# A two-layer hybrid kernel: 23 added constant products in the opening, and two of its three order tables written anew

## The reference, cut to what matters

```python
x = x + conv(group_norm(x))           # 16 graphs of 256 nodes, 16 features, 16 times
    # E = softmax(V_e @ sigmoid(..)), S = softmax(V_s @ sigmoid(prod2 + b_s), axis=1)
    # out = sum_k (cheb[k] * S).T @ x @ Theta[k]; relu; conv over time; + residual; layer norm
t = x as tokens                        # (16, 256 tokens, 256 channels)
t = t + linear_attention(layer_norm(t))   # 16 heads, causal, phi = elu + 1
t = t + ffn(layer_norm(t))                # shared part and top 4 of 16 experts
```

## Time and profile before

| what | value |
|---|---|
| median of 3 runs | 1003.73 us (1002.51 to 1003.75) |
| the profiled execution | 1005.99 us, its span 1004.2 us |
| granted clock, mean over the span | 0.952 |
| PE busy | 941.5 us, 94% |
| DVE busy | 606.8 us, 60% |
| ACT busy | 426.0 us, 42% |
| POOL busy | 210.2 us, 21% |
| the chain that ended last | PE 86%, DVE 6%, ACT 6% |
| first product of `0:gu0` | 188.43 us into the span |

### The profile page before, as it was taken

How to read it: one execution, slowest core, us unless ns; L and a number is a source line. 1 busy time by engine, 2 the same in 40 slices (tenths; PEclk the granted TensorE clock), 3 DMA queues, 4 the chain that set the end, 5 groups by cost and what they waited for, 6 DMA issues and landing times.

```text
span 1004.2 us, 20050 instructions
## 1 busy us (share of the span) xinstructions
PE 941.5 (94%) x8208; PEld 832.8 (83%) x8208; DVE 606.8 (60%) x1630; ACT 426.0 (42%) x808; POOL 210.2 (21%) x184
## 2 busy tenths in 40 slices
PE   4797779999999999999999999999999999999997
PEld 2586556998988989889888898889888888988997
DVE  5548854667576366853777447853768447854532
ACT  3533413452365325741265424752256513632442
POOL 2003200022312023111331123121231113212222
PEclk9689757999999999999999999999999999999999
DMA  9100000000000000000000010000100000000000
GB/s 321 45 1 22 1 1 1 2 23 12 1 11 1 1 33 1 12 1 32 2 12 2 1 33 1 12 2 1 33 1 12 2 12 2 11 1 12 12 12 11
DMA packets 14378, 17.78 MB, mean 18 GB/s; under 512 B 1072, under 2 KB 12720, under 8 KB 14288
## 3 DMA queue, kind: packets, MB, share of 16 engines
q1 hardware_dynamic: 14288, 16.51, 4.9%
HBM read 12.31 MB, written 4.19 MB: 16 GB/s over the span
## 4 chain that ended last, share of the span: by engine, by line
PE 86%; DVE 6%; ACT 6%; issue 1%; POOL 0%; DMA 0%; POOLq 0%; SPq 0%; DVEq 0%; ACTq 0%
PE ring L1305 9%; PE g_ps L501 5%; PE d_ps L501 5%; PE d_ps L503 4%; PE d_ps L502 4%; PE g_ps L503 4%; PE g_ps L502 4%; PE u_ps L501 4%; PE u_ps L502 4%; PE u_ps L503 4%; PE ring L1177 4%; PE num L1206 3%; PE ring L1288 3%; PE ring L501 3%; PE ring L503 3%; PE ring L502 3%
## 5 line engine op out<-in xcount | busy, mean ns | idle before, releaser
L647 POOL TENSOR_TENSOR hl<-hb,hh 128x512 fp32r<-128x512 f32 x96 | 127.2, 1325 | 494.4 <-ACT hh L791 494.4
L1145 DVE TENSOR_TENSOR hb<-sl,u_ps 128x512 f32<-128x512 f32 x88 | 60.2, 684 | 99.9 <-PE u_ps L503 48.4
L791 ACT ACTIVATE hh<-hb 128x512 fp32r<-128x512 f32 x96 | 60.8, 633 | 140.1 <-DVE hb L1149 119.7
L501 PE MATMUL d_ps<-hh,down_h 128*128 128x256 f32 x384 | 114.9, 299 | 1.9 <-POOL hl L647 1.9
L501 PE MATMUL g_ps<-normed_h,gate_h 128*128 128x256 f32 x352 | 109.0, 310 | 3.6 <-DVE scb L1061 3.5
L503 PE MATMUL d_ps<-hh,down_l 128*128 128x256 f32 x384 | 107.5, 280 | 0.0
L502 PE MATMUL d_ps<-hl,down_h 128*128 128x256 f32 x384 | 107.4, 280 | 0.0
L503 PE MATMUL g_ps<-normed_h,gate_l 128*128 128x256 f32 x352 | 100.4, 285 | 0.0
L501 PE MATMUL u_ps<-normed_h,up_h 128*128 128x256 f32 x352 | 100.1, 284 | 0.0
L502 PE MATMUL g_ps<-normed_l,gate_h 128*128 128x256 f32 x352 | 100.1, 284 | 0.0
L502 PE MATMUL u_ps<-normed_l,up_h 128*128 128x256 f32 x352 | 100.1, 284 | 0.0
(11 more groups left out here) (338 smaller groups left out, 2176.3 us busy)
## 6 DMA issues: line engine op xcount, KB each, us to landing
out_x<-kept SPq DMA_DIRECT2D x16, 256.0 KB, 2.1
x_s<-in_x SPq DMA_DIRECT2D x14, 256.0 KB, 3.0
raw_weights<-in_gateT SPq DMA_DIRECT2D x4, 384.0 KB, 9.2
raw_weights<-in_upT SPq DMA_DIRECT2D x4, 384.0 KB, 10.1
raw_weights<-in_down SPq DMA_DIRECT2D x4, 384.0 KB, 12.6
cheb_s<-in_cheb SPq DMA_DIRECT2D x3, 256.0 KB, 4.8
raw_weights<-in_wqkvT SPq DMA_DIRECT2D x2, 384.0 KB, 6.9
shared<-in_x SPq DMA_DIRECT2D x2, 256.0 KB, 2.9
```

Source lines behind the costliest of these rows:

```text
L501: eng.matmul(ps, wh, xh, start=start, stop=False, **how)
L647: pool.tensor_tensor(hl[:, j % 2, :], hb, hh[:, j % 2, :].bitcast(F32), ALU.subtract).then_inc(*ffn_pool.mark(p, f"lo{j}"))
L791: act.activation(hh[:, j % 2, :], hb, ACT.Copy).then_inc(*ffn_act.mark(p, f"hi{j}"))
L1145: dve.tensor_tensor(hb, sl, gate_up(p, j)[1][:, :], ALU.mult).then_inc(*ffn_dve.mark(p, f"h{j}"))
```

## The change

A new chain `warm` has 23 steps `hot0` to `hot22`, each one float32 product of the identity with 256 columns of the constants into `g_ps`, which nothing reads; `gu0` overwrites the bank later. A hot step exists on PE alone, waits for nothing of its own and signals nothing. All 23 stand in `OPENING`, before `0:gu0`. `OPENING` and `BODY` are written anew; `CLOSING` and all other work stay as they were.

```diff
+CHAINS["warm"] = [f"hot{i}" for i in range(23)]
 OPENING = """
-    0:gn 0:xg 1:gn 1:xg 0:xT0 0:M 1:xT0 0:xT1 1:M 0:Y0 0:prod 1:xT1 0:xb 0:Epre 1:Y0 0:Eexp 1:prod 0:Erep 0:lr 1:Epre
...
+    0:gn 1:gn 0:xg 0:hot0 0:hot1 0:hot2 1:xg 0:hot3 0:xT0 0:M 0:xT1 0:Y0 0:hot4 0:prod 0:hot5 1:xT0 0:Epre 1:M 0:hot6
+    0:Eexp 1:xT1 1:Y0 0:hot7 1:prod 1:Epre 0:Erep 1:Eexp 0:lr 0:p2 0:sp0 0:rv0 1:Erep 0:sp1 1:lr 0:st0 0:rv1 1:p2 0:Y1
...
 BODY = """
-    tok0 tok1 +1 lg +1 nrm gn xl0 xg +1 xl1 +1 xT0 r1 M xT1 +1 k0 +1 k1 v1 r2 +2 r3 Y0 +1 q0 v0 kt q1 prod silu r4 +2
...
+    +1 tok0 tok1 lg nrm +1 gn +2 xg xl0 +1 xl1 +1 r1 +2 xT0 M k0 k1 v1 xT1 +1 Y0 r2 q0 r3 v0 kt q1 prod silu +1 r4 +1
...
             def front(p, name):
+                if name in CHAINS["warm"]:
+
+                    pe.matmul(g_ps[:, 0:N], ident, cs[:, 0:N], start=True, stop=True)
+                    return
                 g = room(p)
```

More of the change, by code:

```diff
@@ new lines @@
+    0:Eexp 1:xT1 1:Y0 0:hot7 1:prod 1:Epre 0:Erep 1:Eexp 0:lr 0:p2 0:sp0 0:rv0 1:Erep 0:sp1 1:lr 0:st0 0:rv1 1:p2 0:Y1
+    0:hot8 0:st1 1:sp0 0:xb 1:rv0 0:o0 0:o1 1:sp1 0:tc0 1:st0 0:tc1 1:rv1 0:z1 1:xb 0:z2 1:Y1 0:hot9 0:z3 1:st1 1:o0
+    1:o1 1:tc0 0:tok0 1:tc1 1:z1 0:tok1 0:hot10 2:gn 0:nrm 0:hot11 1:z2 0:xl0 0:xl1 0:hot12 0:hot13 2:xg 0:k0 0:k1
+    0:v1 2:xT0 2:M 0:q0 0:v0 0:kt 0:q1 0:hot14 0:hot15 0:hot16 1:z3 2:xT1 0:hot17 0:dent 2:Y0 0:hot18 2:prod 0:kv
+    2:Epre 2:Eexp 0:rd 0:S00 0:hot19 0:hot20 2:Erep 0:V00 0:S01 0:at0 2:lr 0:V01 0:S10 2:p2 0:V10 0:S11 2:sp0 0:V11
@@ L123 @@
+    2:rv0 0:at1 2:sp1 2:st0 0:wo0 0:wo1 2:rv1 2:Y1 0:hot21 0:tk0 0:exp 0:tk1 0:nrm2 2:st1 2:o0 0:xn0 0:hot22 1:tok0
+    0:xn1 1:tok1 2:o1 0:lg 1:nrm 0:r1 +1 0:r2 1:xl0 1:xl1 +1 2:tc0 +1 0:r3 0:silu 1:k0 1:k1 1:v1 1:q0 1:v0 1:kt 1:q1
+    +1 2:tc1 0:r4 1:dent 1:kv +1 0:cb +2 1:rd +4 1:S00 +1 1:V00 +3 1:S01 +1 1:at0 1:V01 +1 2:xb +2 1:S10 +2 1:V10 +2
+    1:S11 +2 1:V11 +3 1:at1 +1 2:z1 +1 1:wo0 +1 2:z2 +2 1:wo1 +3 1:tk0 1:tk1 +3 1:nrm2 +2 2:z3 +1 1:xn0 +2 1:xn1 +2
+    1:exp +1
 """
 BODY = """
-    tok0 tok1 +1 lg +1 nrm gn xl0 xg +1 xl1 +1 xT0 r1 M xT1 +1 k0 +1 k1 v1 r2 +2 r3 Y0 +1 q0 v0 kt q1 prod silu r4 +2
@@ L127 @@
-    Epre dent cb kv +1 rd +2 Eexp S00 +2 Erep +1 lr +3 p2 +2 sp0 rv0 sp1 +1 st0 V00 +2 rv1 Y1 +3 xb S01 +1 st1 +1 at0
-    +1 o0 +1 o1 V01 +1 S10 +1 tc0 +1 tc1 V10 z1 S11 +1 V11 +2 at1 +1 z2 +1 wo0 +1 wo1 +2 tk0 tk1 +5 nrm2 z3 +1 xn0 xn1
+    +1 tok0 tok1 lg nrm +1 gn +2 xg xl0 +1 xl1 +1 r1 +2 xT0 M k0 k1 v1 xT1 +1 Y0 r2 q0 r3 v0 kt q1 prod silu +1 r4 +1
+    Epre dent cb kv +1 rd +2 Eexp S00 +2 Erep +1 lr +3 p2 +2 sp0 rv0 sp1 +1 st0 V00 +2 rv1 Y1 +3 S01 +2 st1 +1 at0 +1
+    xb +1 o0 o1 tc0 V01 S10 +1 tc1 V10 z1 +1 S11 +1 V11 +2 at1 +1 z2 wo0 wo1 +2 tk0 +2 tk1 +2 nrm2 +2 z3 +2 xn0 xn1
@@ L165, in program @@
         put(int(word.split(":")[0]) if ":" in word else None, word.split(":")[-1])
-    names = [n for c in CHAINS for n in CHAINS[c]]
-    assert sorted(out) == sorted((p, n) for p in range(PAIRS) for n in names)
+    once = [(p, n) for p in range(PAIRS) for c in CHAINS if c != "warm" for n in CHAINS[c]]
+    assert sorted(out) == sorted(once + [(0, n) for n in CHAINS["warm"]])
     for c in CHAINS:
+        if c == "warm":
+            continue
         orders = [[n for q, n in out if q == p and n in CHAINS[c]] for p in range(PAIRS)]
@@ L194 @@
 GROUPS = [f"{b}{lc}" for b in range(2) for lc in range(2)]
-NO_TILE = ["xg", "Eexp", "rv0", "rv1", "nrm", "nrm2", "at0", "at1", "exp", "silu"] + ["V" + g for g in GROUPS] + CHAINS["tail"] + CHAINS["ffn"] + "lg r1 r2 r3 r4 cb".split()
+NO_TILE = ["xg", "Eexp", "rv0", "rv1", "nrm", "nrm2", "at0", "at1", "exp", "silu"] + ["V" + g for g in GROUPS] + CHAINS["tail"] + CHAINS["ffn"] + CHAINS["warm"] + "lg r1 r2 r3 r4 cb".split()
 RING = 4
```

## The result

Four runs of the changed kernel took 985.80 to 989.00 us, median 987.22 us; the kernel before had a median of 1003.74 us beside them. The ratio is 0.984 (95% interval 0.9825 to 0.9857). The profiled execution took 988.29 us with a span of 986.5 us, 17.7 us under the profiled execution of before (1005.99 us). The mean granted clock rose from 0.952 to 0.980.

What follows compares the result with a forecast made beforehand. Bound: the start of feed-forward work (188.43 us) plus nearly fixed PE work. Opening -8.7 and middle -5.5 sum to -14.2 us, from 1005.99 to 991.8, against the median 989.5, said as 990; range 979 to 999.

Steps and rivals of the forecast that it cites:

- rival 2: Whole kernel: the clock holds everywhere, in 24.4 to 58.5 us too, 9.5 us more gain, 980 us; chance 0.16.
- the prediction's own signs of being wrong: Clock mostly full between 24 and 58 us (then nearer 980), or score groups still at 2.09 us (then 997 or more).
- Its signs for the scores: From 110 to 165 us: clock over 0.8 instead of 0.6, `S` at 1.15 us in at least three of four groups.
- Up to 68 us: Opening, `conv` of pair 0: 24.4 to 44.9 us stays at half clock, DVE's `1:M` delays `0:Eexp`; +1.0 us.
- 68 to 95 us: Opening: hot9 saves 1.7 us at the fall at 79.0, `0:z3` on DVE gives back most; -0.5 us.
- 95 to 123 us: Norm and projections of pair 0: `0:xl0` about 2.5 us later, projections mostly at full clock; sum -2.0 us.
- The scores: 123 to 161 us, scores and weighing: about 8.5 us gained, two falls of 3.4 us take back 2.5; -6.0 us.
- 161 to 188 us: End of the opening: hot21 and hot22 save 1.7 us, one product of 0.5 stands on the path; -1.2 us.
- The middle: Behind `gu0`: waits of `gu0` -3.5, `M` -1.5, half the clock falls -2.5, new waits 2; -5.5 us.
- PE idle by 4 to 5 us less: Sign for the middle: PE idles 4 to 5 us less, with the wait on L1061 gone.
- Rival 1: Whole kernel: the clock falls where it fell before, terms from 95 us on worth 2, middle 4; 997 us; chance 0.20.
- Rival 3: Opening: late DVE and POOL queues (`1:z1`, `2:gn`; `1:M`) cost 5.0 us, products don't raise the clock; 1012 us; chance 0.06.

Runs made afterwards that it cites:

- e3_gn_later: The changed kernel with `gn` of the middle's table moved behind two more feed-forward steps; 1013.24 us.
- e4_eexp_first: The changed kernel with only `Eexp` of pair 0 put back ahead of the work of `M` of pair 1 on DVE; 987.46 us.
- e1_no_hot: The changed kernel without its 23 hot products, both new tables kept; 1000.83 us.
- e4_more_hot: The changed kernel with more hot products in the waits of the opening, 64 in all; 980.64 us.
- e2_norm_first: The changed kernel with the norm of pair 0 put back ahead of `1:z1` and `2:gn`, and `0:Eexp` ahead of `1:M`; 991.73 us.
- e1_new_opening: The changed kernel with the old table for the middle, its new opening and products kept; 988.41 us.
- e1_new_body: The kernel before with the new table for the middle, old opening, no hot products; 999.70 us.
- e1_hot_only: The kernel before with the 23 hot products between the same neighbours, both old tables otherwise kept; 997.61 us.

## Why the prediction held, point by point

990 us was forecast and 987.22 measured. The way the change was said to work came about, on the side of rival 2. That the number came so near has some luck in it: the opening gave 14.0 us in the profiles where 8.7 were forecast (`gu0` at 174.5 us, not 179.5), the middle 3.8 where 5.5 were, and the two misses partly cancel. And one of the prediction's own signs of being wrong came: between 24 and 58 us the clock is mostly full, 0.80 on the mean where it was 0.60. Its signs for the scores came as well: 0.91 from 110 to 165 us, three groups of four at 1.15 us, and the wait on L1061 gone.

**What bounds it.** That the time is the start of `gu0` plus a nearly fixed remainder held in every kernel but e3_gn_later: behind `gu0` lie 809.9 to 815.8 us, while `gu0` itself moves by 22 us.

**Up to 68 us: this step failed.** "So I leave the stretch 24.4 to 44.9 at half clock" gave +1.0; the trace has -3.6. After, only 29.5 to 39.9 and 50.0 to 53.4 us are at half clock, 14 us in place of 27. `Erep` is 2.2 us later (28.33 against 26.12), but not for the reason given, the work of `M` ahead of `Eexp` on DVE: without it (e4_eexp_first) it starts no sooner, since `1:Epre` now stands ahead of it on PE and waits for ACT. It runs in 1.06 instead of 1.86 us, `p2` starts only 1.4 us later, and the 12.8 us of `o` shrink to 10.5, since the low stretch no longer meets them. `o` starts 0.4 us later than before, with `sp0` of pair 1 (1.9 us at full clock) now ahead of it and no longer behind, which is most of the rest. The clock came back 5 us earlier than in before, at 39.9 instead of 44.9. The reason given, "what holds PE there is not PE", was true of the waits and wrong of the clock. The size is not one number: the four other profiles give -0.5 to -3.2, and e1_no_hot, which had 20 us at half clock there without a single product, -1.8. e4_more_hot shows the rest of it: with every wait filled, `o` starts at 49.8 us.

**68 to 95 us.** -0.5 forecast, -0.4 measured.

**95 to 123 us.** -2.0 forecast, -2.7 up to the scores. The sum came out, its first part did not: `xl0` was to be 2.5 us later and starts at 100.69 us, 2.6 earlier than before (103.28). Two things stand behind that. 4.0 us were in hand from the first two terms, which leaves it 1.4 later in its own stretch. And the late norm was real, `xl0` waits 1.73 us for it, but it was not what the projections waited for: with the old order `xl0` comes 1.1 us sooner in its stretch and the first projection 0.8 later (e2_norm_first). The stretch of low clock is still there, 10.2 us in place of 13.6.

**The scores.** -6.0 forecast, -4.7 measured. Of the two falls of 3.4 us that were counted, one came, of 10.2 us, and three groups of four ran at 1.15 us. In another execution of the same opening none came (e1_new_opening). This term is therefore not one number: the clock's pattern changes from run to run, as the spread of 985.8 to 989.0 us with clocks of 0.984 and 0.980 shows.

**161 to 188 us.** -1.2 forecast, -2.5 measured; about 1.0 of it is work of pair 1 (`xl0`, `xl1`) that now stands behind `gu0`, and so is no gain. With it counted where it stood, this stretch gave 1.5 and the middle 4.8.

**The middle: this step was mis-sized, and its parts wrong.** -5.5 forecast, -3.8 measured. The two waits went (3.5 and 1.8 us), the falls of the clock went wholly (-5.1 where -2.5 was counted), and the new waits, put at 2, are 4.1 and 3.4 us. The forecast "PE idle by 4 to 5 us less" is refuted: it idles 1.5 us more. That the falls went because of `w11` and `M` was argued from their place behind those waits; every profile with the new body as it is has none, e1_new_body with the old opening too. But in e1_new_opening, with all five waits for `scb` there, one fall is left of three, so the wait alone does not make them; which move removes them was not tried.

**The rivals.** Rival 1 (997, the clock falls where it fell) is what e1_hot_only measured, 997.6, but for the old order, not the new; its sum leaves out the +1.0 of the first term and would be 998 with it. Rival 2 (980, the clock holds everywhere) was reached by e4_more_hot at 980.64 us: the ceiling was about right, and 23 products are too few for it. Rival 3 fell: the products do raise the clock, and undoing its two late queues gains nothing (e2_norm_first, e4_eexp_first).

**The page's rule.** The Trainium skill (TensorE: Matmul & The Clock Gate, Part 1) puts the cost of the ramp below 1% of a typical span. Here the clock falls again and again while PE waits in the opening, and the kernel in which it no longer falls there is 22.4 us faster, 2.1 to 2.5% by its interval (e4_more_hot), of which the new body had given 4.1 by itself (e1_new_body). For one ramp the rule may hold; for falls that repeat in the waits the measurement decides.

## What to carry to other kernels

Where a profile shows half clock, sum it by stretch and ask what PE waits for there: filling those waits with wide products of constants that nothing reads costs about 0.5 us each at full clock, mostly hides in the wait, and makes all real products in the stretch faster. Fill every wait before the bulk of the work starts, instead of choosing places by where the clock fell in one trace, since the pattern changes between executions; the fill is enough when no stretch is left. Here 23 products were worth 6.2 us in an order that was not made for them and 13.6 in one that was.

On one shared order a removed wait tends to come back at the next consumer (`q0`, then `Y0`), and a step moved later on PE is moved on the engine that feeds it too (`gn`).

## What the runs showed of the hardware

- A product of 16 columns does not hold the clock up and one of 256 does, at the same places and in the same number: 999.4 against 987.2 us.
- The granted clock is not a property of the kernel alone. The same opening gave 34 us at half clock in one profile and 27 in another, at different places; the runs of e1_no_hot spread over 9.9 us, with mean clocks from 0.958 to 0.971, and those of e1_new_opening over 5.6, with 0.978 to 0.986, while e1_hot_only, with falls too, stayed within 0.4, and the kernel without a fall within 1.4.
- The record prints full clock at the start of the span, where the products run at half: the first four hot products of after took 3.76 us together, 0.94 each, under a printed 1.00:

```profile
11.66 3.76 PE L1219 MATMUL g_ps<-constants 128*128 128x256 f32 x8
...
19.62 0.70 PE L1219 MATMUL g_ps<-constants 128*128 128x256 f32 x2
```

- A stretch at half clock does not cost half its length: 48 us less of it brought `gu0` 14 us forward, not 24, and 82 us less 22, not 41. PE was busy for only 67.3 of the 82 us, waits for DVE and ACT take back part, and the added products take their own time; how the difference splits between these was not measured.
